# A third score buffer in the top-p search of a two-layer graph kernel

## What is computed

```python
def _top_p_attention(X, W1, W2, W3):
    logits = (X @ W1.T @ W2.T) @ (X @ W3.T).T
    probs = softmax(logits, axis=-1)
    sp = sorted probs, descending;  cs = cumsum(sp)
    keep = cs - sp < 0.9                       # top-p, per row
    A = probs * keep
    return A / A.sum(-1, keepdims=True)

R = (adj + eye) / row sums
for n in range(2):
    A = _top_p_attention(Xa, W1, W2, W3)
    Xf = R @ Xf
    Xa = A @ Xa
    Z = Z + Xf @ U1[n].T + Xa @ U2[n].T
out = layernorm(X + Z) * ln_g + ln_b           # then x + out, layernorm again
```

## Time and profile before

| | us |
|---|---|
| median of 3 runs | 4354.27 (4349.45 to 4354.54) |
| profiled execution | 4350.77 |
| its span, first to last instruction | 4349.0 |
| PE busy in the span | 3762.5 (87%) |
| DVE busy | 3623.6 (83%) |
| ACT busy | 3114.5 (72%) |
| POOL busy | 1017.3 (23%) |

### The profile page before, as it was taken

How to read it: one execution, slowest core, us unless ns; L and a number is a source line. 1 busy time by engine, 2 the same in 40 slices (tenths; PEclk the granted TensorE clock), 3 DMA queues, 4 the chain that set the end, 5 groups by cost and what they waited for, 6 DMA issues and landing times.

```text
span 4349.0 us, 66313 instructions
## 1 busy us (share of the span) xinstructions
PE 3762.5 (87%) x25364; PEld 3163.1 (73%) x25364; DVE 3623.6 (83%) x6400; ACT 3114.5 (72%) x3128; POOL 1017.3 (23%) x1412
## 2 busy tenths in 40 slices
PE   8677877777777769999999749999999999999996
PEld 5677777777777747777778547777777777778875
DVE  2899999999999939888888188888888889999995
ACT  3789889898989845555555367777777777777771
POOL 0000000000000000001010224444444445555555
PEclk9899999999999989999999979999999999999998
DMA  3211111111111020000000212222233423333332
GB/s 116 93 45 66 45 55 56 47 64 47 64 47 64 27 78 12 19 16 19 16 17 17 87 35 85 87 83 88 88 93 93 134 90 105 107 107 105 100 104 73
DMA packets 131759, 292.49 MB, mean 67 GB/s; under 512 B 14122, under 2 KB 94186, under 8 KB 127058
## 3 DMA queue, kind: packets, MB, share of 16 engines
q1 hardware_dynamic: 131410, 287.99, 20.6%
HBM read 250.19 MB, written 37.75 MB: 66 GB/s over the span
## 4 chain that ended last, share of the span: by engine, by line
PE 34%; ACT 28%; DVE 14%; issue 14%; POOL 10%; DMA 1%; DVEq 0%; SPq 0%; ACTq 0%; POOLq 0%
PE ps L803 11%; PE ps L642 9%; DVE b L1226 7%; ACT b L871 6%; ACT b L988 5%; ACT b L989 5%; DVE b L1173 3%; ACT b L865 3%; PE ps L792 3%; ACT b L971 3%; PE ps L748 3%; PE ps L623 2%; POOL b L468 2%; ACT b L859 1%; PE ps L780 1%
## 5 line engine op out<-in xcount | busy, mean ns | idle before, releaser
L707 PE MATMUL ps<-b 128*128 128x257 f32 x4096 | 902.1, 379 | 0.0
L803 PE MATMUL ps<-b 128*128 128x257 f32 x4096 | 900.9, 379 | 0.0
L642 PE MATMUL ps<-cb,b 128*128 128x128 f32 x4096 | 606.9, 312 | 321.7 <-ACT b L865 321.7
L707 PEld LDWEIGHTS ps<-b 128*128 128x128 f32 x4096 | 775.6, 189 | 118.3 <-issue 3.8
L803 PEld LDWEIGHTS ps<-b 128*128 128x128 f32 x4096 | 770.2, 189 | 111.7
L642 PEld LDWEIGHTS ps<-cb,b 128*128 128x128 f32 x4096 | 546.1, 163 | 371.1 <-ACT b L865 329.6
L1137 DVE SCALAR_TENSOR_TENSOR b<-b 128x4096 f32<-128x4096 f32 x128 | 566.4, 4425 | 63.1 <-ACT b L859 59.8
L1139 DVE CUSTOM_DVE_ANT_0 b<-b 128x4096 f32<-128x4096 f32 x128 | 566.3, 4425 | 5.5 <-DMA b<-in_adj 1.1
L871 ACT ACTIVATE b<-ps 128x1024 f32<-128x1024 f32 x512 | 499.9, 1023 | 75.6 <-PE ps L642 74.0
L623 PE MATMUL ps<-b 128*64 128x128 f32 x8192 | 504.0, 276 | 0.0
L865 ACT ACTIVATE b<-b 128x4096 f32<-128x4096 f32 x128 | 474.4, 3706 | 8.0 <-DVE b L1141 8.0
(11 more groups left out here) (186 smaller groups left out, 4743.2 us busy)
## 6 DMA issues: line engine op xcount, KB each, us to landing
b<-in_adjTb SPq DMA_DIRECT2D x256, 512.0 KB, 3.8
b<-in_adj SPq DMA_DIRECT2D x32, 2048.0 KB, 8.0
y_d<-b SPq DMA_DIRECT2D x64, 128.0 KB, 1.7
h_d<-b SPq DMA_DIRECT2D x64, 128.0 KB, 1.8
b<-h_d SPq DMA_DIRECT2D x64, 128.0 KB, 2.3
b<-in_xT SPq DMA_DIRECT2D x1, 4096.0 KB, 15.8
b<-in_x SPq DMA_DIRECT2D x32, 128.0 KB, 2.2
b<-y_d SPq DMA_DIRECT2D x32, 128.0 KB, 2.1
```

Source lines behind the costliest of these rows:

```text
L642: last = nc.tensor.transpose(bank(2 * (gq % 3), 2)[:, b * 128:(b + 1) * 128], ub[:, u % UB, j * 128:(j + 1) * 128], ident_s)
L707: last = mm(b[:, 0:XA], aj[:, q % AJR, e, :], xf[:, j, :], start=False, stop=(j == NT - 1))
L803: last = mm(o[:, 0:XA], at[:, q % ATR, b, :], xa[:, j, :], start=(j == 0), stop=(j == NT - 1))
```

## The change

The second step gets three score buffers (`eb`, chosen by the new helper `scores(s, t)`, with three sums `zE` read by `zsum(s, t)`); the first step keeps two of them. With the third buffer the following moves, in the second step alone:

- PE makes `logits(n+2)` where it made `logits(n+1)`, and the queries of tile n+3 in `mq`. The queries of tile 2 and the logits of tile 1 are made ahead of the loop, before `Rmul(1)`.
- ACT copies out `logit_ev(n+2)`. `expo` is no longer behind `zx_ev`: `expo(n+2)` stands at the end of `acts`, behind the third level and behind the second `r_ev`. `av_ev` and `mq_ev` stand behind the first level.
- DVE's `rmax` leaves `search` and becomes `rmax(n+2)` in `finish(n)`, between the replacement (1293, 1294) and the wait for `levels`. For tile 1 it stands ahead of level 3 of the search of tile 0.
- POOL's `bracket(n+2)` stands behind `levels(n)` and ahead of `final_add`, where `bracket(n+1)` stood behind `r_post`.

The room for it: `aj` has three chunks in place of four; `junk` is fp8 in place of bf16, with `saturate=False` on its two passes; `u2` holds one step's weights, reloaded between the steps; `gxs` lies on `hin`; `finx` has four rows in place of six, for which SP gets a wait on `f1`; the pads of 8 behind the scores go.

```diff
-    AJR = 4
+    AJR = 3
...
-        eb = r1.take(2, N + 8)
+        eb = r1.take(3, N)
...
-        junk = r1.take(N // 2).bitcast(mybir.dt.bfloat16)
-        u2 = r1.take(2, 2, 256)
+        junk = r1.take(N // 4).bitcast(mybir.dt.float8e4)
+        u2 = r1.take(2, 256)
...
+        def scores(s, t):
+            return eb[:, t % (2 + s), 0:N]
...
+                    if m >= 2:
+                        sp.wait_ge(g["f1"], 2 * (m - 1))
...
                         for p in pairs_in(n - 1):
                             r_post(p)
-                        if n + 1 < NT:
-                            bracket(n + 1)
...
                         if n < NT:
                             levels(n)
+                        if n + 2 < NT:
+                            bracket(n + 2)
                         if n in fslot:
                             final_add(fslot[n])
...
                 logits(0)
                 if s == 1:
+                    pe.wait_ge(s_l1, 16 * 10)
+                    mq(None, 2, zx(None, 2))
+                    logits(1)
                     Rmul(1)
...
-                    if n + 1 < NT:
-                        logits(n + 1)
+                    if n + 1 + s < NT:
+                        logits(n + 1 + s)
...
-                def acts(t, items):
+                def acts(t, items, n):
                     items = list(items)
                     for k in range(1, ACT_LEVELS + 1):
                         if t < NT:
                             level(t, k)
+                        if k == 1:
+                            if 1 <= n <= NT:
+                                av_ev(n - 1)
+                            if n >= 2 or n + 3 < NT:
+                                mq_ev(n - 2 if n >= 2 else None, n + 3 if n + 3 < NT else None)
                         if k >= ACT_LEVELS - 1 and items:
                             r_ev(items.pop(0))
                     for r in items:
                         r_ev(r)
+                    if n + 2 < NT:
+                        expo(n + 2)
...
                         for k in range(ACT_LEVELS + 1 if t else 1, r + 1):
-                            if k == r and t + 1 < NT:
-                                rmax(t + 1)
+                            if t == 0 and k == 3:
+                                rmax(1)
...
                     if s == 1:
                         mark(link, t, 0)
+                        if t + 2 < NT:
+                            rmax(t + 2)
                     ve.wait_ge(g["lr"], t + 1)
```

More of the change, by code:

```diff
@@ L172, in gat_topp_kernel @@
         w8 = r1.take(3, 8)
-        zE = r1.take(2)
+        zE = r1.take(3)
         prs = r1.take(2, XA)
@@ L181, in gat_topp_kernel @@
         hh = r1.take(256)
-        gxs = r1.take(256)
+        gxs = hin
         yr = r1.take(2, 256)
@@ L188, in gat_topp_kernel @@
         fin = r1.take(6, 256)
-        finx = r1.take(6, 256)
+        finx = r1.take(4, 256)
         finz = r1.take(2, 256)
@@ L203, in gat_topp_kernel, with zsum @@
         h_d = nc.dram_tensor("h_d", [N, 256], F32).ap()
+        def scores(s, t):
+            return eb[:, t % (2 + s), 0:N]
+        def zsum(s, t):
+            i = t % (2 + s)
+            return zE[:, i:i + 1]
         def tile_of(d, t):
@@ L333, in _ @@
             ld(u1[:, :, 256:512], U1T[0].rearrange("(k p) n -> p k n", p=128), s_l1)
-            for i in range(2):
-                ld(u2[:, i, :, :], U2T[i].rearrange("(k p) n -> p k n", p=128), s_l1)
+            ld(u2, U2T[0].rearrange("(k p) n -> p k n", p=128), s_l1)
             def chunked(dst, src):
@@ L548, in _ @@
                     bracket(0)
+                    bracket(1)
                 for n in range(LAST + 3 if s else NT + 2):
@@ L769, in mq @@
                         if tz is not None:
-                            last = mm(b[:, 0:256], xz[:, k, :], u2[:, s, k, :], start=(k == 0), stop=(k == 1))
+                            last = mm(b[:, 0:256], xz[:, k, :], u2[:, k, :], start=(k == 0), stop=(k == 1))
                     for k in range(2):
@@ L1041, in _ @@
                 if s == 1:
+                    zx_ev(None, 2)
+                    mq_ev(None, 2)
+                    logit_ev(1)
+                    expo(1)
                     r_ev(1)
@@ L1057, in _ @@
                         zx_ev(tz, tx)
-                    if n + 1 < NT:
+                    if s == 0 and n + 1 < NT:
                         expo(n + 1)
-                    if 1 <= n <= NT:
-                        av_ev(n - 1)
-                    if zm:
-                        mq_ev(tz, tx)
-                    if s == 0 and tx is not None:
-                        gx_ev(tx)
-                    if s == 1:
-                        acts(n + 1, [2 * p + i for p in pairs_in(n) for i in range(2)])
+                    if s == 0:
+                        if 1 <= n <= NT:
+                            av_ev(n - 1)
+                        if zm:
+                            mq_ev(tz, tx)
+                        if tx is not None:
+                            gx_ev(tx)
+                    else:
+                        acts(n + 1, [2 * p + i for p in pairs_in(n) for i in range(2)], n)
                 barrier(ac, kS[s])
@@ L1346, in finish @@
                                            op0=ALU.is_gt if s else ALU.is_ge, op1=ALU.mult).then_inc(g["mask"], 1)
[L1348 removed]
                 eat = {}
[L1350 to L1356 removed]
+                el_at = 2 * (2 if s else 3) + NL // 2
+                eat[0] = el_at
+                if s == 1:
+                    el_at += 2 + NL // 2
+                    eat[1] = el_at
+                for n in range(NT - 1 - s):
+                    el_at += NL // 2 + (NCH if n >= 1 else 0)
+                    eat[n + 1 + s] = el_at
+                    tx = n + 2 + s < NT
+                    el_at += 2 if (n >= 2 or tx) else 0
+                    el_at += 1 if (s == 0 and tx) else 0
                 if s == 0:
```

65 lines of the change are left out of this document (30 added, 35 removed).

## The result

The changed kernel takes 4406.34 us, median of 4 runs (4404.14 to 4408.18), against 4354.02 us for the kernel before on the same chip (4 runs, 4349.45 to 4354.54): a ratio of 1.0122, with the interval 1.0105 to 1.0140. The forecast was 4397 us. The span of the profiled execution grew from 4349.0 to 4405.2, by 56.2 us, where the working gave 45.

What follows compares the result with a forecast made beforehand. No engine bounds the first half; a chain DVE, ACT, POOL, ACT, DVE does. 28 tiles of 57.8 us give +36, start +4, reload +5: +45 on 4350.8, or 4395.8; stated as 4397 us, range 4346 to 4440.

Steps and rivals of the forecast that it cites:

- The tile of the first half: Second step: fourth transposed chunk 6.65 us after the last row, PE's own work 51.15, so 57.8 us a tile.
- The clock: PE, second step: slower granted clock behind stops of 4 us, eight transposes taking 1.97 us instead of some 0.93.
- rival 1: PE, second step: the clock holds in nearly all tiles, 56.0 us each; 4346 us, up to 4360; chance 14%.
- Rival 2: ACT's queue at the last row's end: exponents stay hidden, PE never stops; 4280 us; chance 8%.
- The second half: Second step, later tiles: 57.8 us each there too, with 58 to 59.3 us from mask to mask.
- R: PE, each tile of the second step: the end of the last R @ Xf row, before which exponents cannot start.
- the one on SP: SP's queue: adjacency chunks asked for about 3 us ahead of need, taken at 0; bad end 3 us per tile.
- Rivals 3 and 4: Second half: POOL becomes the bound, 4433 us, 6%. PE's rows: adjacency chunks come late, 4425 to 4480 us, 6%.
- the bad ends: Second step: 59.3 us from mask to mask on POOL and DVE; 3 us per tile for adjacency chunks on SP.
- The reload: Before row 32: PE waits for reloaded Xf and the adjacency chunk queued behind it, 5 us (0 to 10).
- The start: Tile 0: the first bracket falls among five compares, reaching L475 around 2529; PE's fourth chunk 4 us late.
- The parts at nothing: Adjacency ring of three on SP taken at 0; ACT's passes with fp8 output taken as unchanged, 3.71 us.

Runs made afterwards that it cites:

- e1: The changed kernel with ACT making the exponents before it waits for and copies the second R @ Xf row; 4304.21 us, ratio 0.9892.
- d1: The changed kernel with one more ACT pass over half a tile behind the exponents, output thrown away; 4443.61 us, ratio 1.0216.
- e3: The changed kernel with `final_add` ahead of the bracket on POOL and nothing else; 4389.11 us, ratio 1.0089.
- b1: The kernel before with the ring of adjacency chunks cut from four to three; 4349.07 us, ratio 1.0001.
- b2: The kernel before with `junk` in fp8 in place of bf16 and `saturate=False` on its two passes; 4350.31 us, ratio 1.0000.
- e5: e2 with SP asking for a tile's first adjacency chunk ahead of the final rows' stores and loads; 4259.12 us, ratio 0.9792.
- e6: e2 with one adjacency chunk asked for ahead of the final rows' stores, three between stores and loads, the rest behind; 4265.95 us, ratio 0.9804.
- e7: e6 with POOL's bracket behind `r_post`, where the kernel before had it; 4284.53 us, ratio 0.9849.
- e2: e1 with `final_add` ahead of the bracket on POOL; 4267.05 us, ratio 0.9808.

## Why the prediction was right, and where it was off

**The tile of the first half** was right in mechanism and size. Forecast: fourth chunk 6.65 us after the row, stop of 4.0 us, PE's own work 51.15, tile 57.8. Measured: 6.61, 3.99 to 4.00, 57.91 - 6.61 = 51.3, and 57.9. e1 and d1 show that the stop is the cause, by taking it away (51.8 us) and by making it longer (59.7 us). Two things made the sum work: it started from the one event that orders the tile, the end of the row, and it took PE's own work from stretches behind stops of 4 us, with their clock, not from PE's busy time at its best.

**The clock** came out as the forecast, against rival 1, had it: over T1 to T15 the granted clock was 0.96, where it was 0.97 in the kernel before, and each tile showed 0.94 or 0.97. PE's busy time grew from 53.5 to 53.9 us a tile, and its idle time from 3.1 to 4.0. What rival 1 describes was there in e1, at 1.00 over 684 us, and in three tiles of the first half before, behind stops of 1.8, 1.8 and 3.1 us; behind none of the stops of 4.0 us. One sign was wrong: in five of these tiles the eight transposes took only 1.09 us, and the logits behind them were the slow ones (up to 5.40 us).

**Rival 2**, hidden exponents, did not happen, since ACT's queue has the order that it has. e1 is that case made by hand: 4304 us where the rival said 4280. Its first half gained more than the rival had (51.8 us against 53.5, the clock again), its second half less (57.5 us a tile, for chunks).

**The second half** is the term that was too small. I took 57.8 us there too, in three steps: mask at about R, `final_add` within the 58 to 59.3 us from mask to mask, and SP "about 3 us ahead of need, so I take 0". Measured: 58.6 us over 13 tiles, 11.0 us more than forecast. PE waited 8.1 us for chunks in these tiles, 7 times, and 2.1 us for the mask. Behind T29 came the wait of 7.43 us, so that the end took 109.5 us in place of 105.5. The step that failed is the one on SP, the term taken at 0. The slack of 3 us was read with `r_post` behind the bracket; in e3 it is there: in one tile SP has started its last load by 4093.3 us and asks for the chunk at 4095.7, when its slot comes free. But `final_add` was weighed only against the mask, and it stands ahead of `r_post` too. Its own 1.4 us, and the compare of DVE that it releases beside the last step of `r_post`, make `r_post` some 5 us later, and the slack is gone. Rivals 3 and 4, which I had kept apart, meet there, and e3 shows it: POOL's order alone takes the chunk waits away, and 17 us. Together it was inside the bad ends that the working named, and inside the range.

**The reload** was forecast at 5 us over a tile; it was 62.7 - 57.9 = 4.8. A wait of 2.07 us is behind half of it; the row that follows it took 16.10 us in place of 14.08.

**The start** had the wrong sign: +4 forecast, -1.7 measured. This error of 5.7 us hid a third of the 15 us that the second half and the end were over, and that part of the near hit (4397 against 4406) is luck. The step was that the first bracket would come to its ninth step around 2529. It ended at 2522.6:

```profile
2507.68 4.36 POOL L477 TENSOR_SCALAR b<-b 128x1 f32<-128x1 f32 x1
2512.00 0.21 POOL L478 TENSOR_SCALAR b<-b 128x1 f32<-128x1 f32 x1
...
2512.86 4.46 POOL L481 TENSOR_SCALAR b<-b 128x1 f32<-128x1 f32 x1
...
2517.99 4.64 POOL L484 TENSOR_TENSOR b<-b,cb 128x1 f32<-128x1 f32 x1
```

(timeline of POOL, after; the ninth step is L484). Three steps were held for a compare of DVE, the gaps behind the first two let three and two more through, and I had let it fall among five compares. So ACT ended the exponents at 2556.6 and not at 2563.4, and PE made the 32 transposes of tile 0 without a stop. In the steady tile the ninth step ended 17.0 us after R (3031.21 against 3014.17), forecast 17.6; ACT waited for it for 1.73 us there, with nothing lost, as forecast.

**The parts at nothing**: the ring of three and the fp8 output cost nothing alone in the kernel before (b1, b2).

## What to carry to other kernels

When work is moved on an in-order queue, look at the item that it now stands behind and at the one that it stands ahead of: here 4.7 us of exponents that depend on neither sat between a producer's last row and the release of that producer's slot, and one place further up, in the queue's own idle time, they were worth 102 us (4406 against 4304). Where an item is weighed against one deadline, look at everything behind it on its queue as well: `final_add` was in time for the mask and late for `r_post`. And where several queues have slack of a few microseconds each, add the delays along the chain before putting each at zero. Once the first stop is gone, expect the next due item close behind: with the chunks late (e5), the mask late (e6) or the bracket late (e7), a tile of the second half took 54.5, 54.6 and 55.1 us, and reordering one only showed the next.

The best version found is e5, at 4259.12 us, 2.1% below the kernel before and 3.3% below the changed one.

## What the runs showed of the hardware

- Here a stop of 4.0 us in every 58 us cost about half as much again in clock: a tile lost 6.1 us by it, 4.0 idle and 2.1 in slower work. Without stops the granted clock was 1.00 over 684 us.
- POOL's small steps are held while DVE makes a pass with two large inputs, and let through in the gaps of 0.6 us between: a held step shows 4.4 to 4.6 us in place of 0.2 to 0.3 (POOL's timeline of the start above), and two or three more get through in each gap (compare, where one was held).
- POOL idles ahead of the first ordinary instruction behind the maximum over partitions, for nothing that the profile names: 8.32 us ahead of `r_post` in the kernel before, 110.1 us in 14 waits ahead of `final_add` in its second half, and 98.8 us in 13 waits (7.6 us each) ahead of `final_add` in e2, which puts it there again (waits of 3480 to 4200 us):

```profile
POOL b L542 <- issue: 98.8, 13, 8.5
```

- ACT's search pass over 128 x 4096 fp32 takes 3709 ns with an fp8 and with a bf16 output (b2 and before), and the exponents with an fp32 output take 3704 (before).
